# New orders for all four engines in a transformer-block kernel of 16 groups

## Chip, cores and metric

One core of a Trainium2 chip runs the whole kernel in one launch. The metric is the time of one execution on the device in microseconds (us), the median of several runs.

## The reference

The input is x, 32 sequences of 256 tokens with 128 channels, in float32. On it work an attention-like layer (RWKV, with spiking neurons in front and behind) and then a feed-forward network with ternary weights. Cut to what matters:

```
u   = x + lif(time_mix(layer_norm(x)))       # neurons that integrate over time and fire
x3  = u + lif(...)                           # a second set of neurons
y   = x3 + channel_mix(layer_norm(x3))       # k = square(relu(xk @ fWk)); sigmoid(r) * (k @ fWv)

time_mix(x):    xk, xv, xr = x*m + shift(x)*(1-m)
                k, v, r = xk @ Wk, xv @ Wv, xr @ Wr
                running maximum o; A, B = exp(...); nd = sums of A, B*v over time
                sigmoid(r) * (n / d) @ Wo

ffn(y):         f   = layer_norm(y)
                h   = silu(f @ W1 * s1) * (f @ W2 * s2)      # 128 -> 512
                h   = gelu(h @ H1 * s)                       # 512 -> 512
                h   = gelu(h @ H2 * s)                       # 512 -> 512
                out = y + layer_norm(h @ W3 * s3)            # 512 -> 128
```

## The kernel before

The 8192 tokens are cut into 16 groups (G[0] to G[15]) of 512 tokens, two sequences each. Every engine has a list of small named operations, each on one group, nearly always on a tile of 128 x 512. Six groups are under way at any time: while one is in its last matrix, another is loaded. An index is a block of 128 of the 512 hidden features, from 0 to 3, so hidden(2, g, 3) is the fourth block of the product with H2.

No queue or scheduler sets the order of work. Each engine runs its own list, written out by hand-set calls, and a semaphore holds an operation until its input is there: `after(engine, semaphore, n)`. An engine takes its list in line, so one late input holds everything behind it on that engine. The lists have three parts: `opening()`, one body `turn(g)` that runs eight times (i from FIRST = 5 to LAST = 12, with g[k] = G[i - k]), and `ending()`, which is written out for the last groups.

The operations that the text speaks of:

- ScalarE: norm_1, z_1, z_2 (copies of turned tiles with scale and shift), tanh_1 and tanh_2 (sigmoid), under and bounds, exps, log, inverse, relu and square (channel mix), f0 and high (the upper part of a number, in fp32r, at L900), silu (L887), gelu (L906), output_scaled (L914), neuron_input_1 (L852). It loads a table of functions at gelu_table, exp_table and silu_table.
- VectorE: low(layer, g, m) (L289), the rest hid - high, which is float32 minus float32, both in SBUF; swiglu (L1640); fire and fired_flag (L1548, one number copied out of PSUM); add_1 (L1560) and add_2 (L1598), spikes from PSUM plus a tile; stats and moments; mix_1, mix_2, norm_2, numerator (L1519), ratio_end (L1530), sum_over_time (a scan).
- GpSimd (POOL): variance, rstd and offset for the five normalisations, norm_0 (L424, four pieces), shift_1 (L437) and shift_2, weighted_sum (L432), low for some blocks (also L289), residual_5 (L513: y_out = f_out + xres), neurons(...), which is nothing but a test of the flag that fired_flag writes.
- TensorE: k_product, v_product, r_product; channel_k and channel_v; to_gate, to_value, hidden and last_product (L2255; each float32 operand split into high and low, two matmuls per block of 128, so hidden has eight matmuls and waits before each block for its high and its low); turn_1 to turn_5 and spikes_turned (L2216), transposes; fired_sum (L2208).

Each tile of a second hidden layer is written by gelu(1), split by high(2) on ScalarE and by low(2) on GpSimd (blocks 0 and 2) or VectorE (1 and 3), and read by hidden(2).

TensorE's program has one more thing. After its `opening()` it waits for the weights' parts, reads a number that says whether the weights need a third part, and branches to one of two copies of the rest:

```python
program(False, True)
for k in range(len(parts)):
    pe.wait_ge(s_hi_w[k], 1)
    pe.wait_ge(s_lo_w[k], 1)
pe.wait_ge(s_rest_all, 1)
long_weights = pe.value_load(w_rest_all[0:1, 0:1].bitcast(I32))
with pe.If(long_weights != 0):
    program(True, False)
with pe.Else():
    program(False, False)
```

A program called with `first` false runs onset(), the turns and ending(). In this run the number is zero.

Of the kernel before, what the change touches and what calls it, by code (L numbers as in the profile page):

```python
# [62 lines left out]
def build(nc, x_in, vec_in, scale_in, mix_in, ffn_in, out):  # L63
# [13 lines left out]
    with ExitStack() as ctx:  # L77
# [146 lines left out]
        s_e = sem("s_e")  # L224
# [140 lines left out]
        def _(pool):  # L365
# [152 lines left out]
            def opening():  # L518
# [3 lines left out]
                offset_1(G[0])  # L522
                norm_0(G[0])
                shift_1(G[0])
# [11 lines left out]
                rstd(2, G[0])  # L536
                norm_0(G[2])
                shift_2(G[0])
                offset_1(G[2])
# [3 lines left out]
                variance(1, G[3])  # L543
                neurons(1, G[0])
                neurons(0, G[1])
                rstd(1, G[3])
                variance(3, G[0])
                rstd(3, G[0])
                variance(2, G[1])
                rstd(2, G[1])  # L550
                offset_1(G[3])
# [4 lines left out]
                weighted_sum(G[2], 0)  # L556
                offset_3(G[0])
                low(1, G[0], 1)
# [5 lines left out]
                low(2, G[0], 2)  # L564
                variance(3, G[1])
                variance(2, G[2])
# [3 lines left out]
                variance(1, G[4])  # L570
                low(3, G[0], 0)
                variance(4, G[1])
                rstd(4, G[1])
                rstd(1, G[4])
                weighted_sum(G[3], 1)
                offset_1(G[4])
                offset_3(G[1])
                weighted_sum(G[3], 0)
                variance(5, G[0])
                norm_0(G[4])  # L580
                low(1, G[1], 1)
                shift_1(G[4])
                rstd(5, G[0])
                offset_5(G[0])
# [3 lines left out]
                norm_5(G[0])  # L588
                low(2, G[1], 2)
                residual_5(G[0])  # L590
                variance(2, G[3])
                rstd(2, G[3])
                variance(3, G[2])
# [6 lines left out]
                offset_3(G[2])  # L600
# [3 lines left out]
                norm_0(G[5])  # L604
                weighted_sum(G[4], 0)

            def turn(g):

                variance(5, g[4])
                rstd(5, g[4])  # L610
                offset_5(g[4])
                low(1, g[3], 1)
                variance(1, g[-1])
                norm_5(g[4])
                shift_1(g[0])
                neurons(1, g[2])
                neurons(0, g[1])
                low(2, g[3], 0)
                low(2, g[3], 2)
                residual_5(g[4])  # L620
                variance(3, g[2])
                variance(2, g[1])
# [12 lines left out]

            def ending():

                variance(5, G[9])
                rstd(5, G[9])
                offset_5(G[9])  # L640
                low(1, G[10], 1)
                variance(1, G[14])
                neurons(1, G[11])
                shift_1(G[13])
                norm_5(G[9])
                neurons(0, G[12])
                rstd(1, G[14])
                low(2, G[10], 0)
                low(2, G[10], 2)
                variance(2, G[12])  # L650
                rstd(2, G[12])
                variance(3, G[11])
                residual_5(G[9])
                rstd(3, G[11])
                shift_2(G[12])
# [6 lines left out]
                offset_1(G[14])  # L662
                variance(5, G[10])
                rstd(5, G[10])
                offset_5(G[10])
                low(1, G[11], 1)
                neurons(1, G[12])
                shift_1(G[14])
                offset_3(G[11])
                norm_5(G[10])  # L670
                neurons(0, G[13])
                low(2, G[11], 0)
                residual_5(G[10])
                low(2, G[11], 2)
                variance(3, G[12])
                variance(2, G[13])
                rstd(2, G[13])
                rstd(3, G[12])
                variance(1, G[15])
                low(3, G[11], 0)  # L680
                variance(4, G[12])
                shift_2(G[13])
                rstd(4, G[12])
                rstd(1, G[15])
                norm_0(G[15])
                weighted_sum(G[14], 1)
                offset_3(G[12])
                weighted_sum(G[14], 0)
# [6 lines left out]
                shift_1(G[15])  # L695
                residual_5(G[11])
                neurons(1, G[13])
                neurons(0, G[14])
                low(2, G[12], 0)
# [6 lines left out]
                shift_2(G[14])  # L706
                variance(4, G[13])
                offset_3(G[13])
# [3 lines left out]
                variance(5, G[12])  # L712
                rstd(5, G[12])
                low(1, G[13], 1)
                offset_5(G[12])
                norm_5(G[12])
                neurons(1, G[14])
                low(2, G[13], 0)
                neurons(0, G[15])
                residual_5(G[12])  # L720
                low(2, G[13], 2)
                variance(2, G[15])
                variance(3, G[14])
                rstd(2, G[15])
                rstd(3, G[14])
# [9 lines left out]
                neurons(1, G[15])  # L735
                residual_5(G[13])
                low(2, G[14], 0)
                offset_3(G[14])
# [8 lines left out]
                low(2, G[15], 0)  # L747
                variance(5, G[14])
                rstd(5, G[14])
                low(2, G[15], 2)  # L750
# [3 lines left out]
                low(3, G[15], 0)  # L754
# [11 lines left out]
        def _(act):  # L766
# [155 lines left out]
            def opening():  # L922

                norm_1(G[0])
                z_1(G[0])
                high_weights(1)
                high_weights(0)
                gelu_table()
                tanh_1(G[0])
                under(G[0], 1)  # L930
                exp_table()
                bounds(G[0])
                under(G[0], 0)
                exps(G[0], 0)
                exps(G[0], 1)
                norm_1(G[1])
                z_1(G[1])
                log(G[0])
                inverse(G[0])
                high_weights(3)  # L940
                high_weights(2)
                neuron_input_1(G[0])
                rest_weights(1)
                rest_weights(2)
                gelu_table()
                rest_weights(0)
                z_2(G[0])
                bounds(G[1])
                tanh_1(G[1])
                under(G[1], 1)  # L950
                under(G[1], 0)
# [3 lines left out]
                exps(G[1], 0)  # L955
                relu(G[0], 1)
                norm_1(G[2])
                square(G[0], 0)
                square(G[0], 1)
                relu(G[0], 3)  # L960
                square(G[0], 3)
                square(G[0], 2)
                rest_weights(3)
                log(G[1])
                inverse(G[1])
                z_1(G[2])
                gelu_table()
                neuron_input_1(G[1])
# [3 lines left out]
                bounds(G[2])  # L972
                tanh_1(G[2])
                under(G[2], 1)
# [3 lines left out]
                exps(G[2], 0)  # L978
                square(G[1], 0)
                relu(G[1], 1)  # L980
                f0(G[0])
                square(G[1], 2)
                square(G[1], 1)
                relu(G[1], 3)
                log(G[2])
# [4 lines left out]
                square(G[1], 3)  # L990
# [4 lines left out]
                z_1(G[3])  # L995
# [2030 lines left out]
```

## Time and profile before

| | us |
|---|---|
| median of 3 runs | 657.61 (657.49 to 659.11) |
| the profiled execution | 658.89 |
| its span, first to last instruction | 656.9 |
| TensorE busy | 586.7 |
| VectorE busy | 556.3 |
| ScalarE busy | 535.3 |
| GpSimd busy | 418.5 |
| mean clock granted to TensorE | 0.964 of full |

In rows of a timeline the first number is the start in us from the span's first instruction, the second the duration (of the xN instructions together, where several like ones are put in one row), then engine, line, operation, and output <- input. Square brackets at the end give idle time of the engine just before, and who ended it. In rows of windows each engine has its busy time in the stretch, with its count of instructions.

### The profile page before, as it was taken

To read this page: it belongs to the slowest core of one execution; us is meant where nothing else is said; L and a number is where in the kernel's file an instruction comes from. 1 tells how busy PE (TensorE), PEld (TensorE's weight loads), DVE (VectorE), ACT (ScalarE), POOL (GpSimd) and SP (SyncE) were. 2 spreads that over 40 slices of the span, in tenths; PEclk is the share of its full clock that TensorE was granted. 3 is DMA by queue.
4 is the path that set the end of the run, shared out by engine and by line. 5 is a ranking of instruction groups with operands and counts; after the bars stand their busy time and mean duration, and the time that the engine had idled before them with its cause. 6 is when DMAs were issued, how large, how long until landed. Compare 5 with 4: busy or idle time off the path is not lost. (4 is left out here: it accounts for less than half of the span.)

```text
span 656.9 us, 9756 instructions
## 1 busy us (share of the span) xinstructions
PE 586.7 (89%) x2241; PEld 362.5 (55%) x2241; DVE 556.3 (85%) x1538; ACT 535.3 (81%) x849; POOL 418.5 (64%) x571
## 2 busy tenths in 40 slices
PE   1366599999999999999999999999999999999994
PEld 0122247575656666565756566665746666656662
DVE  2978699989999999989999999999999899875543
ACT  4767397979799897979797998979797988958673
POOL 3553346768676777767777767776858665563442
PEclk9659699999999999999999999999999999999998
DMA  8010001001010101010010101010000101000001
GB/s 292 0 33 16 18 1 33 1 18 32 18 32 17 33 17 32 17 33 1 17 33 17 32 18 32 17 33 17 5 29 0 33 0 33 1 16 2 16 1 32
DMA packets 26574, 17.02 MB, mean 26 GB/s; under 512 B 1168, under 2 KB 25744, under 8 KB 26256
## 3 DMA queue, kind: packets, MB, share of 16 engines
q1 hardware_dynamic: 26512, 16.34, 8.2%
q8 instruction: 21, 0.34, 0.2%
q14 instruction: 41, 0.34, 0.2%
HBM read 12.14 MB, written 4.19 MB: 25 GB/s over the span
## 5 line engine op out<-in xcount | busy, mean ns | idle before, releaser
L906 ACT ACTIVATE hid<-p_f,scale 128x512 f32<-128x512 f32 x128 | 87.9, 686 | 65.0 <-PE p_f L2255 64.5
L2255 PE MATMUL p_f<-a_lo,w_hi 128*128 128x512 f32 x320 | 134.1, 419 | 1.6 <-DVE a_lo L289 0.7
L2255 PE MATMUL p_f<-a_hi,w_hi 128*128 128x512 f32 x320 | 125.9, 393 | 0.0
L2255 PE MATMUL p_f<-b_lo,w_hi 128*128 128x512 f32 x256 | 111.4, 435 | 2.3 <-DVE b_lo L289 0.9
L2255 PE MATMUL p_f<-b_hi,w_hi 128*128 128x512 f32 x256 | 100.7, 393 | 0.0
L900 ACT ACTIVATE a_hi<-hid 128x512 fp32r<-128x512 f32 x128 | 79.1, 627 | 2.9 <-DVE hid L1640 1.6
L432 POOL TENSOR_TENSOR nd<-factors,pq 128x512 f32<-128x512 f32 x32 | 38.7, 1209 | 62.9 <-DVE pq L1507 62.9
L289 DVE TENSOR_TENSOR a_lo<-hid,a_hi 128x512 fp32r<-128x512 f32 x96 | 65.7, 704 | 9.4 <-ACT a_hi L900 8.9
L2255 PEld LDWEIGHTS p_f<-a_lo,w_hi 128*128 128x128 f32 x320 | 60.3, 189 | 21.1 <-issue 7.0
L416 POOL TENSOR_TENSOR rstd<-var,minus_half 128x4 f32<-128x4 f32 x64 | 70.0, 1098 | 2.2
L289 POOL TENSOR_TENSOR b_lo<-hid,b_hi 128x512 fp32r<-128x512 f32 x32 | 45.4, 1432 | 38.6 <-DVE fired_all L1548 26.2
L289 POOL TENSOR_TENSOR a_lo<-hid,a_hi 128x512 fp32r<-128x512 f32 x32 | 47.3, 1478 | 35.1 <-ACT a_hi L900 35.1
L2255 PEld LDWEIGHTS p_f<-a_hi,w_hi 128*128 128x128 f32 x320 | 60.4, 189 | 10.7 <-issue 1.2
L2232 PE MATMUL p_m<-mixed,mix 128*128 128x512 f32 x128 | 64.8, 621 | 0.9 <-ACT kk L870 0.9
L2240 PE MATMUL p_m<-kk,mix 128*128 128x512 f32 x128 | 63.3, 595 | 1.6 <-ACT kk L874 1.6
L2255 PEld LDWEIGHTS p_f<-b_lo,w_hi 128*128 128x128 f32 x256 | 48.1, 188 | 27.1 <-issue 16.1
L2255 PEld LDWEIGHTS p_f<-b_hi,w_hi 128*128 128x128 f32 x256 | 48.2, 188 | 13.0 <-issue 3.6
L2164 PE MATMUL p_turn<-ident,n 128*128 128x128 f32 x192 | 31.4, 289 | 20.0 <-ACT n L789 17.7
L2164 PEld LDWEIGHTS p_turn<-ident,n 128*128 128x128 f32 x192 | 22.8, 147 | 45.5 <-issue 43.6
L1466 DVE SCALAR_TENSOR_TENSOR mixed<-d,vec,z 128x512 f32<-128x512 f32 x48 | 34.9, 762 | 9.3 <-POOL d L437 9.3
L424 POOL TENSOR_SCALAR x<-xa,neg_mean,rstd 128x128 f32<-128x128 f32 x64 | 41.5, 660 | 0.3 <-POOL rstd L412 0.3
L900 ACT ACTIVATE b_hi<-hid 128x512 fp32r<-128x512 f32 x64 | 39.9, 630 | 1.7
(143 smaller groups left out, 1437.8 us busy)
## 6 DMA issues: line engine op xcount, KB each, us to landing
xa<-in_x SPq DMA_DIRECT2D x16, 256.0 KB, 2.8
xb<-in_x SPq DMA_DIRECT2D x16, 256.0 KB, 3.0
out<-y_out SPq DMA_DIRECT2D x15, 256.0 KB, 3.3
kk<-in_ffn SPq DMA_DIRECT2D x1, 1024.0 KB, 6.5
hid<-in_ffn SPq DMA_DIRECT2D x1, 1024.0 KB, 8.9
mix<-in_mix SPq DMA_DIRECT2D x1, 512.0 KB, 6.5
gate<-in_ffn SPq DMA_DIRECT2D x1, 512.0 KB, 5.1
mix<-in_mix SPq DMA_DIRECT2D x1, 320.0 KB, 3.8
```

What stands on the lines that cost most here:

```text
L289: eng.tensor_tensor(lo[:, m], hid[:, m], hi[:, m].bitcast(F32), ALU.subtract).then_inc(s_lo[layer][m], 1)
L416: pool.tensor_tensor(rstds[n][:, :], var[n][:, :], minus_half[:, 0], ALU.pow).then_inc(s_rstd[n], 1)
L424: last = pool.tensor_scalar(out_[:, j], in_[:, j], neg_mean[n][:, j:j + 1], rstd[:, j:j + 1], ALU.add, ALU.mult)
L432: pool.tensor_tensor(nd[:, n], factors[:, 0], pq[:, n, :, 0:T], ALU.mult).then_inc(s_apq, 1)
L900: act.activation(dst[:, m], hid[:, m], ACT.Copy).then_inc(s_hi[layer], 1)
L906: act.activation(hid[:, m], p_f[m % 2][:, :], ACT.Gelu, scale=scale[:, 1 + layer, m:m + 1]).then_inc(s_gelu[layer], 1)
L1466: dve.scalar_tensor_tensor(mixed1[:, n], d1[:, :, :], col(("tmk", "tmv", "tmr")[n]), z1[:, :, 0:T], ALU.mult, ALU.add).then_inc(s_mixed1, 1)
L2164: last = pe.transpose(p_turn[:, j * P:(j + 1) * P], tiles[:, j], ident[:, :])
L2232: pe.matmul(p_m[m % 2][:, :], mix[:, MIX["fWk"] + m], flat(mixed2[:, 1]), start=True, stop=True).then_inc(s_fk, 1)
L2240: last = pe.matmul(p_m[0][:, :], mix[:, MIX["fWv"] + m], kk[:, m], start=(m == 0), stop=(m == HB - 1))
L2255: last = pe.matmul(out_, w[:, b], x[:, k], start=(k == 0 and t == 0), stop=(k == n - 1 and t == len(terms) - 1))
```

## The change

No operation is added or taken away, and none goes to another engine. The lists of all four engines are written in a new order, in opening, turn and ending. Two waits name another semaphore of the same kind, since the operation that comes last has changed. The turn begins at another operation on each engine (ScalarE's at relu(g2, 3), VectorE's at low(3, g4, 1), GpSimd's at weighted_sum(g1, 0), TensorE's at hidden(2, g4, 3)), and the code between moved from the turn into opening and ending; this alone does not change the order.

TensorE's test of the weights comes later, by three operations:

```diff
                     spikes_turned(1, G[0])
-
-                def onset():
-
                     after(pe, s_x3, G[0].n)
                     spikes_turned(0, G[1])
                     after(pe, s_fired[0], G[1].n)
                     after(pe, s_h_in[0], G[1].n)
                     k_product(G[2])
-                    after(pe, s_bv[0], G[1].n)
-                    v_product(G[2])
+
+                def onset():
+
                     after(pe, s_z1, G[2].n)
                     turn_2(G[1])
                     after(pe, s_fired_all[0], G[1].n)
                     r_product_1(G[2])
+                    after(pe, s_bv[0], G[1].n)
+                    v_product(G[2])
```

In the turn, on ScalarE:

```diff
                 silu(g[3], 0)
                 silu(g[3], 1)
                 square(g[2], 3)
+                silu(g[3], 2)
                 high(1, g[3], 0)
-                silu(g[3], 2)
+                high(1, g[3], 1)
                 silu(g[3], 3)
-                high(1, g[3], 1)
                 norm_1(g[0])
...
                 gelu(1, g[3], 0)
+                gelu(1, g[3], 1)
                 high(2, g[3], 0)
+                high(2, g[3], 1)
                 neuron_input_1(g[1])
-                gelu(1, g[3], 1)
-                high(2, g[3], 1)
                 gelu(1, g[3], 2)
```

On VectorE:

```diff
+                fire(0, g[1])
                 neuron_input_2(g[2])
                 fire(1, g[2])
-                fire(0, g[1])
+                moments_1(g[-1])
+                mix_1(g[0], 0)
                 fired_flag(1, g[2])
-                mix_1(g[0], 0)
                 mix_1(g[0], 1)
                 mix_1(g[0], 2)
+                low(2, g[3], 1)
                 fired_flag(0, g[1])
                 add_2(g[2])
-                low(2, g[3], 1)
                 stats_3(g[2])
                 add_1(g[1])
                 stats_2(g[1])
                 low(2, g[3], 3)
```

On GpSimd:

```diff
+                weighted_sum(g[1], 0)
+                norm_0(g[0])
                 variance(5, g[4])
                 rstd(5, g[4])
                 offset_5(g[4])
                 low(1, g[3], 1)
-                variance(1, g[-1])
+                offset_3(g[3])
                 norm_5(g[4])
                 shift_1(g[0])
                 neurons(1, g[2])
...
                 low(2, g[3], 0)
                 low(2, g[3], 2)
                 residual_5(g[4])
...
                 low(3, g[3], 0)
+                variance(1, g[-1])
                 rstd(1, g[-1])
                 offset_1(g[-1])
                 weighted_sum(g[0], 1)
-                norm_0(g[-1])
-                weighted_sum(g[0], 0)
-                offset_3(g[2])
```

On TensorE:

```diff
                     after(pe, s_relu[1], g[2].n)
                     channel_k(g[2], 3)
-                    after(pe, s_gate, g[4].n, HB, 4)
-                    v_product(g[1])
+                    after(pe, s_f_cm, g[4].n)
+                    to_gate(g[3], 0)
                     after(pe, s_f0_hi, g[3].n)
                     after(pe, s_f0_lo, g[3].n)
                     turn_5(g[4])
-                    after(pe, s_f_cm, g[4].n)
-                    to_gate(g[3], 0)
+                    after(pe, s_relu[2], g[2].n)
+                    channel_v(g[2], 0)
...
                     hidden(1, g[3], 2)
+                    after(pe, s_x2, g[2].n)
+                    spikes_turned(1, g[2])
                     after(pe, s_fired_all[1], g[2].n)
                     fired_sum(0, g[1])
-                    after(pe, s_x2, g[2].n)
-                    spikes_turned(1, g[2])
                     after(pe, s_gelu[1], g[3].n, HB, 2)
                     hidden(1, g[3], 3)
```

v_product(g[1]) now stands between channel_k(g[2], 0) and channel_k(g[2], 1). In opening and ending the changes are of the same kind, pairs and triples of neighbours in another order; in the opening ScalarE loads its gelu table first, and VectorE and ScalarE take sum_over_time(G[0], 0) and square(G[0], 0) at other places.

## Rows read from the trace of the kernel before

**Rows 1.** The page: busy time of the engines.

```profile
PE 586.7 (89%) x2241; PEld 362.5 (55%) x2241; DVE 556.3 (85%) x1538; ACT 535.3 (81%) x849; POOL 418.5 (64%) x571
```

**Rows 2.** Windows, one loop turn and three turns behind: busy of PE, PEld, DVE, ACT, POOL.

```profile
229.93:266.07 36.14, 35.65 (x141) 22.26 (x140) 33.68 (x96) 32.16 (x54) 26.64 (x36) 1.00 0.08 23
...
446.77:559.51 112.74, 106.83 (x422) 68.25 (x421) 103.99 (x272) 97.67 (x157) 77.66 (x102) 1.00 0.06 17
```

**Rows 3.** Timeline of ScalarE, two stretches of that turn.

```profile
243.86 0.63 ACT L900 ACTIVATE b_hi<-hid 128x512 fp32r<-128x512 f32 x1
244.40 0.58 ACT L852 ACTIVATE h_in<-p_k 128x512 f32<-128x512 f32 x1
...
259.01 0.69 ACT L906 ACTIVATE hid<-p_f,scale 128x512 f32<-128x512 f32 x1
```

**Rows 4.** Timeline of VectorE and TensorE around hidden(1).

```profile
240.67 1.29 DVE L289 TENSOR_TENSOR a_lo<-hid,a_hi 128x512 fp32r<-128x512 f32 x2 [0.26 <-ACT a_hi L900]
...
242.12 0.46 PE L2255 MATMUL p_f<-a_lo,w_hi 128*128 128x512 f32 x1
...
244.49 0.18 PE L2208 MATMUL p_m<-fired,ones 128*128 128x1 bf16 x1
```

**Rows 5.** Timeline of VectorE up to low(2,3).

```profile
246.79 0.14 DVE L1548 COPY fired_all<-p_m 1x1 f32<-1x1 f32 x1
...
247.53 0.68 DVE L289 TENSOR_TENSOR b_lo<-hid,b_hi 128x512 fp32r<-128x512 f32 x1
...
249.06 0.69 DVE L1560 TENSOR_TENSOR x<-p_spk,x 128x512 f32<-128x512 bf16 x1
...
250.58 0.67 DVE L289 TENSOR_TENSOR b_lo<-hid,b_hi 128x512 fp32r<-128x512 f32 x1
```

**Rows 6.** Timeline of GpSimd, the same stretch.

```profile
247.64 2.96 POOL L289 TENSOR_TENSOR b_lo<-hid,b_hi 128x512 fp32r<-128x512 f32 x2 [2.89 <-DVE fired_all L1548]
250.56 1.86 POOL L513 TENSOR_TENSOR y_out<-f_out,xres 128x512 f32<-128x512 f32 x1
```

**Rows 7.** Timeline of TensorE: spikes_turned(0), hidden(2,0), r_product_1.

```profile
248.63 0.40 PE L2216 MATMUL p_spk<-ident,spikes 128*128 128x128 bf16 x4
...
251.40 0.47 PE L2255 MATMUL p_f<-b_lo,w_hi 128*128 128x512 f32 x1
...
256.04 1.02 PE L2183 MATMUL p_m<-mixed,mix 128*128 128x512 f32 x2
```

**Rows 8.** Timeline of the ending: VectorE, then GpSimd.

```profile
503.34 1.82 DVE L289 TENSOR_TENSOR b_lo<-hid,b_hi 128x512 fp32r<-128x512 f32 x1
...
503.31 1.30 POOL L513 TENSOR_TENSOR y_out<-f_out,xres 128x512 f32<-128x512 f32 x1
```

**Rows 9.** Timeline of the opening: VectorE, then GpSimd.

```profile
60.11 1.41 DVE L1530 TENSOR_TENSOR yr<-nd,y 128x512 f32<-128x512 f32 x1
...
59.91 1.06 POOL L437 TENSOR_TENSOR d<-z 128x512 f32<-128x512 f32 x1 [1.36 <-ACT z L798]
```

**Rows 10.** Timeline of TensorE behind the test of the weights.

```profile
68.98 0.59 PE L2216 MATMUL p_spk<-ident,spikes 128*128 128x128 bf16 x4 [4.10 <-issue]
...
73.78 2.05 PE L2183 MATMUL p_v<-mixed,mix 128*128 128x512 f32 x2 [2.41 <-DVE mixed L1466]
75.62 1.06 PE L2164 MATMUL p_turn<-ident,n 128*128 128x128 f32 x4
```

**Rows 11.** Timeline of VectorE and ScalarE behind the test.

```profile
69.60 0.69 DVE L1560 TENSOR_TENSOR x<-p_spk,x 128x512 f32<-128x512 bf16 x1 [3.09 <-PE p_spk L2216]
...
73.55 1.11 DVE L1450 TENSOR_SCALAR n<-x,mv,rstd 128x128 f32<-128x128 f32 x4
...
76.72 0.78 ACT L857 ACTIVATE z<-p_turn,vec 128x512 f32<-128x512 f32 x1 [1.29 <-PE p_turn L2164]
...
90.66 0.69 ACT L887 ACTIVATE gate<-p_f,scale 128x512 f32<-128x512 f32 x1
```

**Rows 12.** Window of the opening: busy times, then the granted clock.

```profile
63.95:77.60 13.65, 6.93 (x19) 3.19 (x19) 9.65 (x35) 3.12 (x7) 4.62 (x8) 0.50 0.05 13
```

More of the change, by code:

```diff
@@ L569, in opening @@
                 shift_2(G[2])
-                variance(1, G[4])
-                low(3, G[0], 0)
                 variance(4, G[1])
                 rstd(4, G[1])
+                low(3, G[0], 0)
+                variance(1, G[4])
                 rstd(1, G[4])
                 weighted_sum(G[3], 1)
+                norm_0(G[4])
+                weighted_sum(G[3], 0)
+                offset_3(G[1])
+                variance(5, G[0])
+                rstd(5, G[0])
                 offset_1(G[4])
[L577 to L580, printed above, removed]
+                offset_5(G[0])
                 low(1, G[1], 1)
+                norm_5(G[0])
                 shift_1(G[4])
-                rstd(5, G[0])
-                offset_5(G[0])
                 neurons(1, G[2])
@@ L1318, in ending @@
                 f0(G[14])
+                output_scaled(G[13])
+                square(G[15], 0)
+                relu(G[15], 3)
+                silu(G[14], 0)
                 square(G[15], 2)
[L1320 removed]
                 square(G[15], 1)
[L1322 to L1324 removed]
+                silu(G[14], 1)
+                high(1, G[14], 0)
+                output_tokens(G[13])
+                high(1, G[14], 1)
                 square(G[15], 3)
[L1326 to L1328 removed]
                 silu(G[14], 2)
[L1330 removed]
                 silu(G[14], 3)
@@ L2003, in ending @@
                 mix_2(G[13], 1)
+                norm_4(G[12])
+                low(3, G[11], 3)
+                low(3, G[11], 1)
+                relu(G[13], 0)
                 low(3, G[11], 2)
-                norm_4(G[12])
-                low(3, G[11], 1)
-                bounds(G[14])
-                relu(G[13], 0)
-                low(3, G[11], 3)
                 sum_over_time(G[14], 1)
@@ L2596, in ending @@
                     turn_5(G[9])
+                    after(pe, s_f_cm, G[9].n)
+                    to_gate(G[10], 0)
+                    after(pe, s_relu[1], G[11].n)
+                    channel_k(G[11], 3)
                     after(pe, s_relu[2], G[11].n)
                     channel_v(G[11], 0)
-                    after(pe, s_f_cm, G[9].n)
-                    to_gate(G[10], 0)
+                    channel_v(G[11], 1)
                     after(pe, s_gelu[2], G[9].n, HB, 4)
@@ L2656, in ending @@
                     channel_k(G[12], 0)
-                    after(pe, s_gate, G[10].n, HB, 4)
-                    v_product(G[13])
                     after(pe, s_tanh_r2, G[12].n)
@@ L2666, in ending @@
                     last_product(G[10])
-                    after(pe, s_relu[1], G[12].n)
-                    channel_k(G[12], 3)
+                    after(pe, s_gate, G[10].n, HB, 4)
+                    v_product(G[13])
                     after(pe, s_f0_hi, G[11].n)
@@ L2671, in ending @@
                     turn_5(G[10])
+                    after(pe, s_relu[1], G[12].n)
+                    channel_k(G[12], 3)
                     after(pe, s_f_cm, G[10].n)
@@ L2717, in ending @@
                     r_product_1(G[14])
+                    after(pe, s_fired[0], G[13].n)
+                    after(pe, s_h_in[0], G[13].n)
+                    k_product(G[14])
                     after(pe, s_gelu[1], G[11].n, HB, 3)
@@ L2741, in ending @@
                     channel_k(G[13], 2)
+                    after(pe, s_relu[1], G[13].n)
+                    channel_k(G[13], 3)
+                    after(pe, s_f_cm, G[11].n)
+                    to_gate(G[12], 0)
                     after(pe, s_f0_hi, G[12].n)
```

787 lines of the change are left out of this document (384 added, 403 removed).

## The prediction

> **What bounds the kernel now.** I read the page first. TensorE is busy 586.7 of 656.9 us, VectorE 556.3, ScalarE 535.3, GpSimd 418.5 [rows 1]. The change moves nothing out of any engine, so what it can win are TensorE's gaps, and what it can lose are new ones. They add to 70.2 us (656.9 - 586.7).
>
> The windows by turn come next [rows 2]. A loop turn lasts 36.14 us with TensorE busy 35.65, and by the timeline one turn is like the next: a fixed cycle. The three turns behind the loop last 112.74 us, 37.6 each. Three regions follow: opening, loop (eight turns), ending.
>
> What sets 36.14? I followed one turn (groups written for the turn in which group 4 is in its second matrix) in the timelines. ScalarE starts the third gelu(2), at 259.01, in the moment hidden(2,3), which follows the product at 256.04, leaves TensorE [rows 3, 7], and from there ScalarE has work back to back through the exps, squares and silus; the windows are cut at output_scaled, 229.93 and 266.07. At the other end VectorE's low(1) waits for ScalarE's high (240.67, 0.26 idle), and TensorE's hidden(1) takes its result at 242.12 [rows 4]. From there TensorE goes without a gap to hidden(2), whose fourth input is late: its matmul starts at 251.40, just behind VectorE's low(2,3), which ends at 251.25 [rows 5, 7]. So the cycle is ScalarE for some 18 us, then TensorE for some 17, with VectorE's low(1,3) and low(2,3) as joints, and each joint is tight.
>
> **The loop turn, part by part.** Both halves of the cycle hold the same operations after the change: ScalarE's half swaps gelu and high, silu and high, relu and f0, and TensorE's swaps a v_product with channel_k and a turn with to_gate. Those swaps are among operations of 0.6 to 1.1 us whose sum on their engine stays, and where their results are needed later than before there is an idle stretch in between: TensorE loses 0.5 us per turn in all [rows 2]. By itself I cost this at 0, between -0.3 and +0.4: not more gain, since TensorE is busy 35.65 of 36.14, and not more loss, since that is one operation of 0.4 us (the fp32r matmul) pushed ahead of a joint.
>
> What does move is the side chain that ends at low(2,3). It is worked out in steps.
>
> (a) high(2,1) now comes behind gelu(1,1) and high(2,0), without neuron_input_1 between. Gelu(1,1) can start when its hidden product ends. The fired_sum behind that starts at 244.49 [rows 4], so at about 244.69. Start to start, ScalarE's gelu costs some 0.57 and high some 0.53 when they queue (a high at 243.86, the next operation at 244.40 [rows 3]); so gelu(1,1) at 244.69, high(2,0) at 245.26, high(2,1) from 245.79 to 246.42.
>
> (b) VectorE now has low(2,1) ahead of fired_flag(0) and add_2 instead of behind them. It is free for it at 246.45 instead of running the flag at 246.79 [rows 5]. So low(2,1) is at 246.45, 0.60 start to start, and the flag at 247.05 to 247.19 instead of 246.93.
>
> (c) GpSimd's low(2,0) stands behind that flag: it started at 247.64, 0.71 after the flag's end [rows 5, 6]. It moves to 247.90.
>
> (d) Before, its first 0.6 us met VectorE's low(2,1) (247.53 to 248.21), and the pair low(2,0), low(2,2) took 2.96 us [rows 6]; such an operation alone takes 1.30 [rows 8], and 1.27 from start to start (the next one starts 0.03 before the end of the first). Now VectorE is on add_2 and statistics, which stood beside GpSimd's second low before without lengthening it. So the pair takes 2.54 and ends at 250.44 instead of 250.60.
>
> (e) residual_5 follows it, at 250.40 instead of 250.56.
>
> (f) VectorE's low(2,3) does not move: it is behind add_1 and stats_2, and add_1 starts at 249.06 because TensorE's spikes are only turned at 248.63 to 249.03 [rows 7]. TensorE's order up to there holds the same work. It stays at 250.58.
>
> So GpSimd's residual_5 would start 0.18 us before VectorE's low(2,3), where now it starts 0.02 us before. That matters because of what the trace shows of such pairs. Both operations read two SBUF tensors. At 0.02 us VectorE gets through (0.67 us) and GpSimd takes 1.86 [rows 5, 6]. In the ending the same two operations meet at 503.31 and 503.34: GpSimd's takes its 1.30, and VectorE's takes 1.82, that is until 505.16, 0.55 behind GpSimd's end [rows 8]. In the opening ratio_end starts 0.20 behind a shift and takes 1.41 [rows 9], where two SBUF tensors alone take 0.67 [rows 5]. They exclude each other, the first one in wins, and with a lead of 0.18 the first one is GpSimd. Then low(2,3) lasts until 250.40 + 1.30 + 0.55 = 252.25, TensorE's matmul starts at 252.40 instead of 251.40, and nothing behind it can be drawn forward, since TensorE takes its orders in line and was gapless from there to 259.01. Price: **+1.0 us per turn**, eight turns, **+8.0 us**. Bounds: 0 where VectorE still wins, and +1.15 (1.82 - 0.67, all of it on the path) times eight, +9.2. I take 8.0, as (a) to (f) are each good to some 0.05 us and the lead is 0.18. As VectorE and GpSimd both hang on the same cycle, the pair meets again in each turn in the same way.
>
> The Trainium skill says this outright ("SBUF — State Buffer", section "SBUF: two separate sides"): a VectorE operation with two SBUF inputs and a GpSimd operation that reads SBUF take an exclusive lock on shared ports, and whichever starts first keeps it for the whole instruction. The trace agrees: 1.82 us for an operation of 0.67. By the rule the change costs the 8.0; without it the sum would stand below zero.
>
> Other meetings, costed at nothing: numerator (235.9) may now meet the last piece of norm_0, which GpSimd runs behind weighted_sum instead of before it. A piece of norm_0 has 0.66 us and VectorE would lose at most that, ahead of swiglu(2); it has 0.26 us of idle time before low(1,2) as cover [rows 4]. Without cover it is +0.3 per turn, which the range holds. Low(1,1) and the later variance(1) and offset_3 lie on GpSimd, which is idle for 9.5 us of the turn [rows 2].
>
> **The opening.** TensorE's test of the weights stands between the two spikes_turned: the engine idles 4.10 us before 68.98 [rows 10]. Everything of groups 0 to 2 queues behind: VectorE's add_1 waits 3.09 us (69.60), and z_2(G1) waits for the turn on TensorE at 75.62 (76.72) [rows 10, 11]. After the change the spikes and k_product(G2) come first, so add_1 starts at about 66.5 (69.60 - 3.09), and k_product runs from 65.3 to 67.3, for some 2.0 us as v_product at 73.78 [rows 10]. The 4.1 us of the test follow, to 71.4, while VectorE and GpSimd do add_1, statistics and norm_2, which took from 69.60 to 74.66, 5.1 us [rows 11], and so end near 71.6. The turn now stands ahead of v_product; I put it at 72.2 instead of 75.62, and z_2 at 73.3 instead of 76.72: 3.4 us won. Some of it goes again. Between 63.95 and 77.60 the clock granted is 0.50 [rows 12], and products that now run behind 77.60 fall into it; a pair takes 2.05 us there (73.78 [rows 10]) against 1.02 (256.04 [rows 7]). One pair on the path is 1.0, of which I count 0.9: -2.5. And between 30 and 52 us there is a small loss, as sum_over_time(0) and the squares of group 0 come later; it lies in idle time of TensorE and costs at most 0.5. The term is **-2.5**. Bounds: 0, if what releases silu at 90.66 is another chain, and -4.1, the whole gap. The rest of the opening, behind silu at 90.66, is much like a loop turn; I leave it unchanged.
>
> **The ending.** Its six turns are set out by hand; the first three take 1.4 us more than a loop turn each, 4.3 in all [rows 2]. Part of that is the meeting at 503 (1.15) and others like it. Following the new order by hand, group 10's low(1,3) comes 0.2 earlier, and group 11's silus some 1.2 earlier; behind that the meetings of VectorE and GpSimd are luck. I take **-1.0**, with bounds -4.3 (all three turns like a loop turn) and +2 (two more meetings of 1.0). The last chain, from output_scaled(G15) to the store, keeps its order.
>
> **The sum.** -2.5 + 8.0 - 1.0 = +4.5 on a span of 656.9: 661.4. The profiled execution took 658.9 with 2.0 outside the span, and lies 1.3 above the median of the runs, 657.6. A profile taken in the same way would show about 663.4; the median follows with 657.6 + 4.5 = **662.1 us**. Changes below 0.3% (2 us) are about what a measurement of this kernel can't tell from no change.
>
> **The rivals.**
> *A, the race is not lost.* Low(2,3) keeps its 0.67 us. For it: the lead is worked out to 0.18 from steps of 0.05 each, and VectorE now wins at 0.02. Then -2.5 + 0 - 1.0 = -3.5: 654.1. It decides if GpSimd's pair of lows ends at 250.55 or later, or if VectorE reaches low(2,3) by 250.42. This ends on the other side.
> *B, the gains of the opening are taken up elsewhere.* The race is not lost, but numerator meets norm_0 (+0.3 per turn, +2.4), or the opening wins nothing: -3.5 + 2.4 = -1.1 to -1.0: 656.5. For it: norm_0 does move to just there. Against it: idle time lies behind it.
> *C, more meetings than one.* The race is lost, numerator's too (+2.4), and the ending has +2 instead of -1: -2.5 + 9.2 + 2.4 + 2 = +11: 668.7; with one of the two, about 665.
> *D, the lock settles otherwise.* The turn grows by 1.0, but TensorE's delay shifts the pair apart in the next turn, so every other turn pays: +4 - 3.5 = +0.5: 658.1. Against it: the turns of before repeat.
>
> **How the numbers follow.** The forecast has 0.43, C 0.12, A 0.28, B 0.11, D 0.06. The forecast's own range, with the opening between -4.1 and 0 and the ending as said, is 659.7 to 665.5. To hold 8 in 10 the range must take in A, whose middle is 654.1 and which reaches to about 652; at the top it takes in part of C: 652 to 666. Slower by over 0.3% (above 659.6): forecast and C, 0.55. Faster (below 655.6): A and a bit of B, 0.30. Within: B's rest and D, 0.15.
>
> **What would show it.** In the profile after, the gap of 4.10 us on TensorE stands behind k_product(G2), and silu(G0,0) starts at about 88.2 instead of 90.66. The loop turn, from one output_scaled to the next, is 37.1; VectorE's low(2,3) takes about 1.7 us and GpSimd's residual_5 1.30; TensorE's fourth block of hidden(2,0) waits more than 1 us. If the turn is still 36.1 and residual_5 still takes 1.86, A is right. If the turn is longer with low(2,3) at 0.67, another joint has slipped and my account of the loop is wrong. If silu(G0,0) is not earlier, the test was not on the path.

## The result and the profile after

The changed kernel takes 663.39 us (median of 4 runs, 663.14 to 664.39), beside 658.36 for the kernel before on the same chip: 1.0087 times as long, with a 95% interval of 1.0064 to 1.0111. The forecast was 662.1, slower. The span of the profiled execution is 661.6 us; it was worked out to 661.4. Two executions were far slower than all others of their kernels and are in no ratio: one of the kernel before with 682.8 us and one of the kernel with the test late, below, with 2583 us; why is not known.

The page first: busy time of the engines in the changed kernel. It answers to [rows 1].

```profile
PE 585.7 (89%) x2241; PEld 363.7 (55%) x2241; DVE 566.4 (86%) x1538; ACT 533.9 (81%) x849; POOL 404.3 (61%) x571
```

The reader is to see that the same 1538 instructions of VectorE are busy 10 us longer and the same 571 of GpSimd 14 us shorter. Nothing was added, so VectorE stands in something that GpSimd stood in before.

Windows of the changed kernel, cut at output_scaled as before; the columns are start and end, length, and then busy time of PE, PEld, DVE, ACT and POOL. They answer to [rows 2]. The first two are neighbouring loop turns, the last is the three turns behind the loop.

```profile
228.44:265.77 37.33, 35.75 (x141) 22.40 (x140) 34.69 (x97) 31.99 (x53) 24.78 (x36) 1.00 0.07 22
265.77:302.08 36.31, 35.75 (x141) 22.33 (x140) 33.79 (x97) 32.01 (x54) 25.05 (x36) 1.00 0.08 23
...
451.79:563.56 111.77, 106.67 (x421) 68.39 (x422) 104.70 (x275) 96.81 (x156) 74.63 (x101) 1.00 0.06 17
```

TensorE is busy 35.75 in both turns, so the long one has 1.0 us more of waiting, and VectorE's busy time holds 0.9 of it. Of the eight turns, seven are long and one is not. That one turn, group 5's, makes the cause plain, for its neighbour runs the same lists. Timelines of the changed kernel, first group 4's turn (VectorE, GpSimd, TensorE), then group 5's (the same); they answer to [rows 5 to 7].

```profile
245.15 0.67 DVE L289 TENSOR_TENSOR b_lo<-hid,b_hi 128x512 fp32r<-128x512 f32 x1
245.75 0.14 DVE L1548 COPY fired_all<-p_m 1x1 f32<-1x1 f32 x1
...
249.19 1.77 DVE L289 TENSOR_TENSOR b_lo<-hid,b_hi 128x512 fp32r<-128x512 f32 x1
...
246.63 2.52 POOL L289 TENSOR_TENSOR b_lo<-hid,b_hi 128x512 fp32r<-128x512 f32 x2 [3.57 <-DVE fired_all L1548]
249.11 1.30 POOL L513 TENSOR_TENSOR y_out<-f_out,xres 128x512 f32<-128x512 f32 x1
...
251.10 0.47 PE L2255 MATMUL p_f<-b_lo,w_hi 128*128 128x512 f32 x1 [1.10 <-DVE b_lo L289]
...
283.08 0.14 DVE L1548 COPY fired_all<-p_m 1x1 f32<-1x1 f32 x1
...
286.48 0.78 DVE L289 TENSOR_TENSOR b_lo<-hid,b_hi 128x512 fp32r<-128x512 f32 x1
...
284.19 2.52 POOL L289 TENSOR_TENSOR b_lo<-hid,b_hi 128x512 fp32r<-128x512 f32 x2 [3.80 <-ACT b_hi L900]
286.67 1.75 POOL L513 TENSOR_TENSOR y_out<-f_out,xres 128x512 f32<-128x512 f32 x1
...
287.41 0.47 PE L2255 MATMUL p_f<-b_lo,w_hi 128*128 128x512 f32 x1
```

In group 4's turn GpSimd's residual_5 starts 0.08 before VectorE's low(2,3) (249.11, 249.19). It takes its 1.30, low(2,3) takes 1.77, and TensorE waits 1.10 us with that operation named as the one that ended the wait. In group 5's turn GpSimd's low(2,0) starts 1.0 us behind the flag's end instead of 0.7, residual_5 comes 0.19 behind low(2,3), low(2,3) takes 0.78, and TensorE does not wait.

The opening, TensorE then VectorE and ScalarE, answers to [rows 10, 11].

```profile
62.80 0.59 PE L2216 MATMUL p_spk<-ident,spikes 128*128 128x128 bf16 x4 [0.59 <-POOLq L471]
64.17 0.60 PE L2216 MATMUL p_spk<-ident,spikes 128*128 128x128 bf16 x4 [0.79 <-DVE x L1598]
64.57 2.02 PE L2183 MATMUL p_k<-mixed,mix 128*128 128x512 f32 x2
69.94 1.09 PE L2164 MATMUL p_turn<-ident,n 128*128 128x128 f32 x4 [3.35 <-DVE n L1450]
...
64.99 0.67 DVE L1560 TENSOR_TENSOR x<-p_spk,x 128x512 f32<-128x512 bf16 x1
...
71.07 0.78 ACT L857 ACTIVATE z<-p_turn,vec 128x512 f32<-128x512 f32 x1 [3.28 <-PE p_turn L2164]
87.02 0.69 ACT L887 ACTIVATE gate<-p_f,scale 128x512 f32<-128x512 f32 x1
```

The 3.35 us in which TensorE waits before 69.94 are put down to VectorE's norm_2, so the test, which falls in them, no longer shows. In the trace its load and its branch run from 65.21 to 69.03, and norm_2 ends at 69.80: the test is over before it.

Cut at silu(., 0), the span's 4.64 us (661.55 less 656.91) are these. Silu(G0,0) moves from 90.66 to 87.02: -3.64. From there to silu(G2,0): -0.20. The eight turns from silu(G2,0) to silu(G10,0) take 298.48 instead of 289.72: +8.76. The rest takes 204.70 instead of 204.98: -0.28.

### The profile page after: what moved, and what is told of

Its sections match the earlier page's. It is cut to its first block and busy times, and to the rows that moved or that the text cites. A ratio compares the mean times of both kernels' runs of the same rounds, so it can differ in the third digit from the quotient of the medians.

```text
span 661.6 us, 9756 instructions
## 1 busy us (share of the span) xinstructions
PE 585.7 (89%) x2241; PEld 363.7 (55%) x2241; DVE 566.4 (86%) x1538; ACT 533.9 (81%) x849; POOL 404.3 (61%) x571
## 5 line engine op out<-in xcount | busy, mean ns | idle before, releaser
L416 POOL TENSOR_TENSOR rstd<-var,minus_half 128x4 f32<-128x4 f32 x64 | 73.9, 1160 | 1.5
L289 POOL TENSOR_TENSOR b_lo<-hid,b_hi 128x512 fp32r<-128x512 f32 x32 | 42.0, 1325 | 45.0 <-DVE fired_all L1548 26.7
L289 POOL TENSOR_TENSOR a_lo<-hid,a_hi 128x512 fp32r<-128x512 f32 x32 | 44.4, 1387 | 30.6 <-ACT a_hi L900 30.5
L442 POOL TENSOR_TENSOR d<-z 128x512 f32<-128x512 f32 x16 | 16.6, 1040 | 40.5 <-ACT z L857 40.5
```

Source lines behind the costliest of these rows:

```text
L289: eng.tensor_tensor(lo[:, m], hid[:, m], hi[:, m].bitcast(F32), ALU.subtract).then_inc(s_lo[layer][m], 1)
L416: pool.tensor_tensor(rstds[n][:, :], var[n][:, :], minus_half[:, 0], ALU.pow).then_inc(s_rstd[n], 1)
L442: pool.tensor_tensor(d2[:, :, :], z2[:, :, 1:T + 1], z2[:, :, 0:T], ALU.subtract).then_inc(s_d2, 1)
```

## The experiments

Two theories stood against each other for the loop: the race for shared ports between residual_5 and low(2,3), and worse lists of ScalarE and TensorE by themselves. For the opening: the test's place, and the other new orders. "Lead" is the time by which residual_5 starts ahead of low(2,3). All but three runs edit only the loop's turn; the others move the test.

**One 0.2 us operation ahead of residual_5.** The changed kernel with

```diff
                 low(1, g[3], 1)
-                offset_3(g[3])
                 norm_5(g[4])
...
                 low(2, g[3], 2)
+                offset_3(g[3])
                 residual_5(g[4])
```

> The changed kernel with one 0.20 us operation of GpSimd, offset_3(g[3]), moved in the turn from behind low(1, g[3], 1) to between low(2, g[3], 2) and residual_5(g[4]). Theory (the race for the shared ports costs the loop 1.2 us per turn): residual_5 started 0.07 to 0.09 us before VectorE's low(2,3) in six turns; with 0.15 to 0.20 us put before it, it starts behind, low(2,3) takes 0.67 to 0.78 again and residual_5 1.75 to 1.86, every loop turn is 36.1 to 36.4 us instead of 37.33, and the median is 654 to 656, some 8 below the changed kernel's 663.4. Rival (the loop is longer because ScalarE's and TensorE's lists are laid worse): the turn stays at 37.3 and the median at 663, or 1 to 2 above for the later offset.

Measured: 658.07 us, 0.9999 times the kernel before (0.9985 to 1.0012), span 655.3 instead of 661.6. Six turns take 36.17 to 36.25 us, the last two 37.53 and 38.27. Timeline of this kernel, GpSimd and VectorE in group 4's turn (won) and group 8's (lost):

```profile
245.83 0.19 POOL L488 TENSOR_TENSOR c<-neg_mean,rstd 128x4 f32<-128x4 f32 x1
245.98 1.80 POOL L513 TENSOR_TENSOR y_out<-f_out,xres 128x512 f32<-128x512 f32 x1
...
245.96 0.68 DVE L289 TENSOR_TENSOR b_lo<-hid,b_hi 128x512 fp32r<-128x512 f32 x1
...
390.94 1.30 POOL L513 TENSOR_TENSOR y_out<-f_out,xres 128x512 f32<-128x512 f32 x1
...
391.00 1.80 DVE L289 TENSOR_TENSOR b_lo<-hid,b_hi 128x512 fp32r<-128x512 f32 x1
```

In group 4's turn VectorE starts first by 0.02 and wins, in group 8's GpSimd does, by 0.05. The same lists give 36.2 us in the one case and 37.5 in the other, so the theory of worse lists falls, but for the some 0.07 us by which the won turns stay above 36.14. The median is 2 us above the 654 to 656 expected: the shift was about 0.08 instead of 0.15 to 0.20, and two turns stayed lost.

**The same operation moved elsewhere.** The changed kernel with offset_3 behind shift_1 instead of behind low(1, g[3], 1).

> The same operation moved as well, but to before neurons(1, g[2]), where GpSimd goes idle anyway: residual_5 keeps its start. Theory: the race is lost as before, turn 37.3, median 663 within 1. Rival (what matters is that offset_3 leaves its old place behind low(1, g[3], 1)): the turn gets shorter here just as when it stands ahead of residual_5, median 654 to 656.

Measured: 662.51 us, ratio 1.0062 (1.0039 to 1.0085), span 660.0. As a control it did not hold still: the leads fell from 0.07 to between -0.12 and 0.05 in six turns (0.19 in the other two), three turns were won (36.2 to 36.3 us) and five lost (37.3 to 38.1). Timeline of this kernel, group 4's turn and group 6's, VectorE then GpSimd:

```profile
248.77 0.67 DVE L289 TENSOR_TENSOR b_lo<-hid,b_hi 128x512 fp32r<-128x512 f32 x1
...
248.76 1.85 POOL L513 TENSOR_TENSOR y_out<-f_out,xres 128x512 f32<-128x512 f32 x1
...
321.23 1.80 DVE L289 TENSOR_TENSOR b_lo<-hid,b_hi 128x512 fp32r<-128x512 f32 x1
...
321.19 1.30 POOL L513 TENSOR_TENSOR y_out<-f_out,xres 128x512 f32<-128x512 f32 x1
```

With a lead of 0.01 us VectorE gets through, with 0.04 it does not. Which turn is long goes by the lead again, not by where offset_3 stands.

**Two pieces of the side chain in the kernel before.**

```diff
                 gelu(1, g[3], 0)
+                gelu(1, g[3], 1)
                 high(2, g[3], 0)
+                high(2, g[3], 1)
                 neuron_input_1(g[1])
-                gelu(1, g[3], 1)
-                high(2, g[3], 1)
...
+                mix_1(g[0], 0)
                 fired_flag(1, g[2])
-                mix_1(g[0], 0)
                 mix_1(g[0], 1)
                 mix_1(g[0], 2)
+                low(2, g[3], 1)
                 fired_flag(0, g[1])
                 add_2(g[2])
-                low(2, g[3], 1)
```

> The kernel before, and in its turn only two pieces of the change: ScalarE's gelu(1,1), high(2,0), high(2,1), neuron_input_1 in the new order, and VectorE's mix_1(0) ahead of fired_flag(1) and low(2,1) ahead of fired_flag(0). Theory: these alone bring residual_5 ahead of low(2,3), by 0.05 to 0.2 us; low(2,3) takes 1.7 to 1.8, the turn is 37.1 to 37.4, the median 666 to 668, 8 to 9 above the kernel before. Rival (the loss needs the whole new order, GpSimd's and TensorE's too): turn 36.1 to 36.3, median within 2 of the kernel before.

Measured: 658.65 us, ratio 1.0018 (0.9998 to 1.0037), turns of 36.3. My expectation failed and its rival held: residual_5 starts behind low(2,3), by 0.2 in most turns, and no turn is lost. Timeline of this kernel, VectorE and GpSimd in group 4's turn:

```profile
243.71 0.75 DVE L1466 SCALAR_TENSOR_TENSOR mixed<-d,vec,z 128x512 f32<-128x512 f32 x1 [0.89 <-POOL d L437]
...
245.76 0.67 DVE L289 TENSOR_TENSOR b_lo<-hid,b_hi 128x512 fp32r<-128x512 f32 x1
246.37 0.14 DVE L1548 COPY fired_all<-p_m 1x1 f32<-1x1 f32 x1
...
242.64 1.04 POOL L437 TENSOR_TENSOR d<-z 128x512 f32<-128x512 f32 x1
```

The first mix_1 waits 0.89 us for GpSimd's shift_1, so low(2,1), the flag and residual_5 are late. Something of GpSimd's new order had to be in it.

**A third piece.** The kernel above with GpSimd's variance(1, g[-1]), three small instructions, moved from ahead of norm_5 and shift_1 to behind low(3, g[3], 0), as in the change.

> The kernel before with the two pieces of the side chain (ScalarE's gelu(1,1) and highs, VectorE's mix_1(0) and low(2,1)) and a third: GpSimd's variance(1, g[-1]) moved from ahead of norm_5(g[4]) to behind low(3, g[3], 0), as in the change. With the first two alone residual_5 started 0.2 behind low(2,3), since mix_1(0) waited for GpSimd's shift_1. Theory (that variance is what held shift_1, mix_1(0), the flag and so residual_5): shift_1 is 0.3 to 0.5 earlier, residual_5 leads low(2,3) by 0.05 to 0.3 us, low(2,3) takes 1.6 to 1.8, the turn is 37.1 to 37.4 and the median 8 to 9 above the kernel before. Rival (the lead needs something else of the order too): turn 36.1 to 36.3, median within 2.

Measured: 664.25 us, ratio 1.0105 (1.0080 to 1.0130), span 661.8. At leads of 0.17 to 0.18 six turns take 37.12 to 37.15 us and the last 37.74 (36.74 in the kernel before); group 5's takes 36.16 at a lead of -0.08. The timeline in group 4's turn, VectorE then GpSimd:

```profile
244.54 0.15 DVE L1548 COPY fired_all<-p_m 1x1 f32<-1x1 f32 x1
...
246.26 0.69 DVE L289 TENSOR_TENSOR b_lo<-hid,b_hi 128x512 fp32r<-128x512 f32 x1 [0.23 <-ACT b_hi L900]
...
250.40 1.69 DVE L289 TENSOR_TENSOR b_lo<-hid,b_hi 128x512 fp32r<-128x512 f32 x1
...
250.23 1.31 POOL L513 TENSOR_TENSOR y_out<-f_out,xres 128x512 f32<-128x512 f32 x1
```

Now low(2,1) waits for ScalarE's high, as steps (a) and (b) had it. Three pieces out of the whole change suffice for most of its loss in the loop: the eight turns from silu(G2,0) to silu(G10,0) take 296.73 us, 7.0 more than before, where the whole change costs 8.8. By the ratio the median is 6.9 above the kernel before, a little less than the 8 to 9 expected.

**The test late in the kernel before.**

```diff
                     spikes_turned(1, G[0])
-
-                def onset():
-
                     after(pe, s_x3, G[0].n)
                     spikes_turned(0, G[1])
                     after(pe, s_fired[0], G[1].n)
                     after(pe, s_h_in[0], G[1].n)
                     k_product(G[2])
+
+                def onset():
+
```

> The kernel before with TensorE's test of the weights moved behind spikes_turned(0, G[1]) and k_product(G[2]), and nothing else. Theory (the opening's gain of 3.8 us in the changed kernel is mostly the test's): add_1(G1) 3 us earlier, silu(G0,0) 2.5 to 3.5 us earlier than 90.66, the loop as before at 36.14, median 2.5 to 3.5 below the kernel before. Rival (the gain is that of the other new orders in the opening, which brought spikes_turned(1, G0) 1.5 us forward, and the half clock eats the test's): less than 1 us.

> The kernel before with TensorE's test late once more, beside these two on one chip, as the version to beat: ratio to the kernel before 0.993 to 0.996 as in its first run (0.9937).

Measured: 655.26 us (654.93 without the execution of 2583) and ratio 0.9937 (0.9912 to 0.9961) the first time, 654.75 and 0.9960 (0.9944 to 0.9976) the second: 4.1 and 2.6 us less than the kernel before. Silu(G0,0) starts at 87.14 and 85.47 in the two profiles, and the loop turn stays at 36.13 to 36.18. This kernel beats both others.

**The test early in the changed kernel**, the reverse edit.

> The changed kernel with TensorE's test of the weights put back to where it was, ahead of spikes_turned(0, G[1]) and k_product(G[2]). Theory (the test's place is worth what it was worth in the kernel before, 3.2 to 3.5 us): silu(G0,0) at 90.0 to 90.7 instead of 87.0, the loop as in the changed kernel, median 3 to 3.5 above it, 666.5. Rival (the other new orders of the opening had their own gain of 1.5 us): silu(G0,0) at 88.5 to 89.5.

Measured: 668.66 us, ratio 1.0171 (1.0147 to 1.0196), which is 5.3 us above the changed kernel (5.5 by the two ratios, each good to some 1.6 us); silu(G0,0) is at 91.78. That is 2 us more than the larger of the two expectations in the median and 1.1 us more at silu(G0,0). Timeline of TensorE in this kernel, where the test stands in the second row's idle time:

```profile
63.24 0.55 PE L2216 MATMUL p_spk<-ident,spikes 128*128 128x128 bf16 x4 [0.58 <-POOLq L471]
69.74 0.58 PE L2216 MATMUL p_spk<-ident,spikes 128*128 128x128 bf16 x4 [5.95 <-issue]
```

Idle time is 5.95 us instead of 4.10 [rows 10]. The changed VectorE list has rest_flag, the number that the test waits for, behind stats_3(G[0]): it starts at 64.94 in the changed kernel, 1.5 us behind spikes_turned(1, G[0])'s end. With the test early the number is written at 65.34 and loaded at 65.64, 2.4 us behind the start of spikes_turned(1, G[0]); in the kernel before it lay ready and was loaded 0.5 us behind it. That is what makes the idle time 1.85 us longer. So the late flag is affordable only with the late test; the late test alone does no harm, as the kernel above shows.

**Both offset_3 and variance(1, g[-1]) ahead of residual_5** in the changed kernel.

> The changed kernel with two operations of GpSimd, offset_3(g[3]) and variance(1, g[-1]), some 0.7 us, between low(2, g[3], 2) and residual_5(g[4]). With offset_3 alone six of the eight turns were won by 0.01 to 0.7 us and two lost at a lead of 0.05. Theory: residual_5 now starts 0.3 us or more behind low(2,3) in every turn, all eight turns are 36.1 to 36.3, the span is 653 to 654 and the median 655 to 656. Rival (the longer list of GpSimd moves the loss elsewhere, to variance(2), norm_2 and r_product): turns of 36.5 to 37, median 658 to 662.

Measured: 658.38 us, ratio 1.0022 (1.0010 to 1.0035). No turn is lost (residual_5 is 1.25 behind), but turns take 36.6. Timeline of this kernel, GpSimd then VectorE:

```profile
246.85 0.58 POOL L399 TENSOR_SCALAR var<-mv 128x4 f32<-128x4 f32 x1
247.51 0.20 POOL L400 TENSOR_SCALAR var<-mv 128x4 f32<-128x4 f32 x1
247.79 0.20 POOL L405 TENSOR_TENSOR neg_mean<-mv,minus_one 128x4 f32<-128x4 f32 x1
247.94 1.30 POOL L513 TENSOR_TENSOR y_out<-f_out,xres 128x512 f32<-128x512 f32 x1
...
250.78 0.35 DVE L1450 TENSOR_SCALAR n<-x,mv,rstd 128x128 f32<-128x128 f32 x1 [0.93 <-POOL rstd L416]
```

The rival held. Variance starts 0.16 behind low(2,3) (246.69 to 247.36) and is itself held up by it (0.58 us for an instruction of 0.20; low(2,3) keeps its 0.68). Residual_5 is so late that it ends 0.74 us later in the turn than with offset_3 alone, variance(2) and rstd(2) behind it are late with it, and norm_2 waits 0.93 instead of 0.21. TensorE is 0.33 us later at the transpose that waits for norm_2, which is nearly all of the 0.36 between this turn and the 36.21 with offset_3 alone.

**Variance back in the changed kernel**, with VectorE's moments_1(g[-1]), which it needs; and the same with offset_3 ahead of residual_5.

```diff
                 low(1, g[3], 1)
+                variance(1, g[-1])
                 offset_3(g[3])
                 norm_5(g[4])
...
                 low(3, g[3], 0)
-                variance(1, g[-1])
                 rstd(1, g[-1])
...
                 sum_over_time(g[1], 1)
+                moments_1(g[-1])
                 relu(g[2], 2)
...
                 fire(1, g[2])
-                moments_1(g[-1])
                 mix_1(g[0], 0)
```

> The changed kernel with one piece undone: GpSimd's variance(1, g[-1]) again behind low(1, g[3], 1) and VectorE's moments_1(g[-1]), which it needs, again behind sum_over_time(g[1], 1). It is the mirror of the kernel before with variance moved away, where that piece gave residual_5 its lead of 0.18. Theory: shift_1 and with it residual_5 are 0.2 to 0.5 later, residual_5 starts 0.15 us or more behind low(2,3), the race is won in all eight turns, the turn is 36.2 to 36.5, the span 653.5 to 656 (661.6 less 6 to 8). Rival (in the new order other things hold residual_5): lead and turn of 37.3 stay.

> As the changed kernel with variance(1, g[-1]) and moments_1(g[-1]) back, and offset_3(g[3]) besides between low(2, g[3], 2) and residual_5(g[4]). Theory: shift_1 is 0.2 earlier than with variance back alone, and residual_5 as far behind low(2,3) as there; turn 36.15 to 36.3, span 653 to 654.5, median 655 to 656, level with the kernel before whose test is late. Rival: a turn of 36.5, as when two operations stood ahead of residual_5.

Measured: 659.28 us and ratio 1.0030 (1.0018 to 1.0043) for the first, 658.85 and 1.0011 (0.9996 to 1.0026) for the second. No turn is lost in either, with leads of -0.44 to 0 and of -0.69 to -1.05, so undoing that piece takes the race away. But the turns are 36.8 and 36.6, not 36.3. Timeline of the first, VectorE then TensorE:

```profile
242.03 0.75 DVE L1466 SCALAR_TENSOR_TENSOR mixed<-d,vec,z 128x512 f32<-128x512 f32 x1 [1.33 <-POOL d L437]
242.70 0.14 DVE L1548 COPY fired_all<-p_m 1x1 f32<-1x1 f32 x1
...
243.66 0.38 PE L2216 MATMUL p_spk<-ident,spikes 128*128 128x128 bf16 x4 [0.25 <-POOLq L471]
```

Mix_1(0) now waits 1.33 for shift_1, the flag behind it is late, and TensorE waits 0.25 in spikes_turned(1), which in the new order stands ahead of fired_sum(0). Set beside group 4's turn with offset_3 alone ahead of residual_5 (36.21), TensorE reaches spikes_turned(1) 0.37 us later in the turn, and another 0.2 come in the first blocks of hidden(2). The cause of those 0.2 was not settled.

## Why the prediction was right, step by step

**The bound, the joints.** Right: the kernel still turns on ScalarE's half and TensorE's half, and the loss came in at the joint low(2,3).

**Steps (a) to (f).** The mechanism was right and the lead off. The forecast was 0.18; the changed kernel has 0.07 to 0.09 in six lost turns and 0.20 in the last of the eight, group 9's. In the kernel before with three pieces, where steps (a) to (f) hold as worked out, it is 0.17 to 0.18, and the turn is 37.1 as forecast. The 0.09 between the two kernels in group 4's turn are step (f)'s: low(2,3) does move, since VectorE's add_1 starts 1.92 us behind the flag in the changed kernel and 2.01 with the three pieces, while GpSimd's part behind the flag takes the same time in both. What the steps missed is that low(2,1) can't be early unless shift_1 is. I had taken VectorE as free at 246.45 because of mix_1's move alone; with that move and ScalarE's alone, residual_5 stayed 0.2 behind. It came right in the whole change because variance(1, g[-1]) left its place, an edit that I had listed among those costed at nothing. That the lead had the right sign was so far luck.

**The price per turn.** +1.0 was forecast; a lost turn costs 1.15 to 1.24 in the changed kernel (37.31 to 37.38 against 36.14), the last 1.43, and the one won turn 0.17. A lost low(2,3) takes 1.65 to 1.80 us; it ends 0.55 behind residual_5, as read from [rows 8], so a smaller lead makes a longer wait. The sum is +8.76 for +8.0, within the bound of +9.2, though only seven of eight turns were lost. The range of 659.7 to 665.5 that the forecast gave itself is not what its named bounds add up to: with 8.0 for the loop, -4.1 to 0 for the opening and -4.3 to +2 for the ending it would be 657.2 to 667.6. The measured time lies in both.

**Who wins.** Over twelve profiles, eight turns each, VectorE got through in all 68 turns with a lead of at most 22 ns (in 26 of them GpSimd did start first, by 6 to 22 ns), and lost in all 28 with a lead of at least 42 ns. None of the 96 fell between. The same pair in the ending narrows the gap: unrounded, the lead in [rows 8] is 27 ns, and in the four other kernels with this ending it is 36 to 44 ns, and VectorE lost all five. By the profile's start times the edge lies between 22 and 27 ns. The forecast rested on the single 0.02 and 0.03 of [rows 5, 6] and [rows 8], and these hold.

**The opening.** -2.5 was forecast; the profiles gave -3.64 to silu(G0,0). Here one pair of profiles says little, and this one flatters the change. In this profile of the kernel before, ratio_end starts behind the shift and takes 1.41 us [rows 9], and so it does in the first with the test late. In the other three with that opening's lists on VectorE and GpSimd it starts 0.64 ahead and takes 0.69, and in all seven with the changed lists it starts ahead too. So up to 0.72 of the 3.64 is that race, which the same lists win in one profile and lose in another. Kernels whose opening is that of before have silu(G0,0) at 90.66, 89.32 and 88.48, those with the changed opening between 86.00 and 87.85 (six profiles, mean 86.8). The difference of the means is 2.7. That the test is the cause is shown by moving it alone, in either direction. That it would be hidden behind add_1 to norm_2 was right. The terms were not: z_2 came 5.65 earlier (71.07 for 76.72) where 3.4 were forecast, and 2.0 of that were gone by silu(G0,0) where I had counted 0.9; I did not trace where they went. Beyond the test, the other orders of the opening gained nothing by themselves that the runs could tell.

**The ending.** -1.0 was forecast within -4.3 to +2, and it is -0.28. The three turns behind the loop went from 112.74 to 111.77 as hoped, and what is behind them gave 0.59 of that back (output_scaled(G9) is 5.02 later than before, output_scaled(G12) 4.05, the end 4.64). I looked for no cause there. The ending is where the forecast was a guess, and its error (0.7 too low) and the loop's (0.8 too low) cancel the opening's (1.1 too high, and 0.2 more behind silu(G0,0)): 661.4 for 661.6 is better than the terms deserve.

**The rivals.** A (race not lost, 654.1) is what the three pieces minus one, and the first experiment in six turns, show: the condition it named, GpSimd's pair ending later, was the right one, and some 0.07 us would have been enough. Its number no run reached: where the race is undone in the changed kernel, in all turns or in six, the medians are 658.1 to 659.3, as two turns stay lost or other waits come up. Numerator and norm_0 (B, C) meet, at about no cost: in group 4's turn numerator starts (234.44) while the third piece of norm_0 is under way (234.20 to 234.64) and takes 0.74 us for 0.68, and the fourth piece takes 0.88 for 0.44. In the last turn of the loop it takes 0.87. D did not happen: lost turns follow on lost turns.

## What to carry to other kernels

Where a GpSimd operation and a VectorE operation with two SBUF inputs start within a tenth of a microsecond of each other in a steady loop, the loop's time is decided by which comes first; list such pairs on the critical path before changing any order, and keep a margin on purpose rather than by luck. Put the long GpSimd operation whose result nobody waits for (here residual_5) where it can only come second, but look at what stands behind it: with residual_5 1.25 us behind, its successors were late and the turn stayed 0.4 above that of before. A test or branch that an engine must make belongs in front of an operation that waits for others anyway, and the number it tests must be early enough for its place.

## What was not expected of the hardware

The race has a sharp edge: 22 ns of lead for GpSimd still lets VectorE in, 27 ns does not. In group 5's turn GpSimd is 0.1 to 0.3 us later against VectorE than in its neighbours (0.7 with offset_3 ahead of residual_5), in every kernel with the new side chain, which turned that turn's race in all three kernels that otherwise lost seven; why that turn, the profiles do not show. Executions of the kernel before spread over 3.5 us: of 23 on the chip of the first four experiments 11 lie at 656.0 to 657.5 and 12 at 658.8 to 659.5. Profiles of an unchanged opening differ by 2.2 us at silu(G0,0). The granted clock of 65 to 80 us is 0.58 in one such profile and 0.62 in the other, that of 35 to 50 us 0.50 and 0.64, so the opening's part at half clock goes with it. At spikes_turned(1, G0) two such profiles (64.29 and 62.03) differ by 2.3, of which 0.72 is the race between ratio_end and the shift; that the clock makes the rest, and that these are the two clusters of executions, was only argued.
